# Column sums of z and of its squares: two TensorE matmuls for each two chunks instead of VectorE's additions

## The reference, cut to what matters

```python
messages = jnp.concatenate([node_rep[src], edge_rep[dst]], axis=-1)
messages = _bn_relu(messages @ W1, g1, b1)        # z = messages @ W1, 50000 x 256
# _bn_relu: mu = mean(z, axis=0), var = var(z, axis=0), relu((z - mu) * rsqrt(var + 1e-5) * gamma + beta)
edge_new = segment_sum(messages, dst)
```

## Time and profile before

| | us |
|---|---|
| median of three executions | 3559.73 |
| the profiled execution, own time | 3567.03 |
| its span, first to last instruction | 3565.2 |
| PE matmuls busy in it | 2424.9 (68%) |
| DVE busy | 2395.4 (67%) |
| POOL busy | 1734.6 (49%) |
| ACT busy | 1352.5 (38%) |

### The profile page before, as it was taken

One profiled execution on the slowest core, in us unless ns is written; L12 is line 12 of the kernel. 1 busy time (PEld: TensorE's weight loads), 2 busy tenths in 40 slices (PEclk: granted clock), 3 DMA queues, 4 the chain that ended last, 5 costly groups with the idle time before them and its releaser, 6 DMA issues. The chain is left out here.

```text
span 3565.2 us, 41686 instructions
## 1 busy us (share of the span) xinstructions
PE 2424.9 (68%) x12339; PEld 1976.6 (55%) x12339; DVE 2395.4 (67%) x4693; ACT 1352.5 (38%) x2800; POOL 1734.6 (49%) x1269
## 2 busy tenths in 40 slices
PE   4668733454555543666621999879999999925998
PEld 3522213454444443444421897469888988923788
DVE  5979945777777778877886544344565566615788
ACT  2268833444444441000000435424434434423776
POOL 0257887776667667888888777730000000042000
PEclk9779865555555555888855999889999999966999
DMA  9993224665555656555533774146545645340355
GB/s 373 351 355 34 22 26 130 174 171 164 165 165 166 172 170 137 133 142 134 143 40 39 202 177 89 1 103 185 175 126 172 185 130 173 118 103 8 109 173 176
DMA packets 338453, 517.84 MB, mean 145 GB/s; under 512 B 145379, under 2 KB 227100, under 8 KB 331580
## 3 DMA queue, kind: packets, MB, share of 16 engines
q1 hardware_dynamic: 190254, 436.41, 38.2%
q0 software_dynamic: 134768, 58.41, 14.2%
q10 hardware_dynamic: 13214, 20.35, 1.7%
HBM read 369.65 MB, written 145.38 MB: 144 GB/s over the span
## 5 line engine op out<-in xcount | busy, mean ns | idle before, releaser
L1133 PE MATMUL banks<-rows_r,lhs_r 128*128 128x448 f32 x3500 | 899.1, 372 | 84.0 <-issue 41.6
L728 POOL DMA_INDIRECT counts<-wts x391 | 637.4, 1630 | 307.9 <-DMA counts<-ring 141.0
L1133 PEld LDWEIGHTS banks<-rows_r,lhs_r 128*128 128x128 f32 x3500 | 667.8, 191 | 152.9 <-issue 74.8
L741 POOL DMA_INDIRECT weights<-wts x391 | 620.9, 1588 | 161.8 <-issue 159.1
L1133 PE MATMUL banks<-ring_r,lhs_r 128*128 128x448 f32 x1750 | 525.8, 370 | 0.0
L749 POOL DMA_INDIRECT reg<-tab_p,w x416 | 406.9, 978 | 217.9 <-issue 122.8
L548 DVE SCALAR_TENSOR_TENSOR ring_r<-ring,dinv,rows_r 128x896 fp32r<-128x896 f32 (+1 forms) x300 | 303.7, 1033 | 309.5 <-ACT rows_r L535 309.3
L1221 PE MATMUL banks<-lhs_r,oT 128*128 x416 | 203.3, 489 | 429.8 <-issue 346.6
L535 ACT ACTIVATE rows_r<-ring,dinv 128x896 fp32r<-128x896 f32 (+1 forms) x300 | 285.0, 951 | 399.3 <-PE banks L1133 342.0
L799 POOL DMA_INDIRECT el<-tab_l,base_i x25 | 24.0, 958 | 796.8 <-DMA tab_l<-reg 789.5
L1221 PEld LDWEIGHTS banks<-lhs_r,oT 128*128 128x128 f32 x416 | 131.9, 317 | 447.3 <-issue 447.0
(11 more groups left out here) (269 smaller groups left out, 4104.6 us busy)
## 6 DMA issues: line engine op xcount, KB each, us to landing
ring<-weights SPq DMA_DIRECT2D x225, 448.0 KB
ring<-counts SPq DMA_DIRECT2D x150, 448.0 KB
zbuf<-reg SPq DMA_DIRECT2D x208, 256.0 KB
reg<-zbuf SPq DMA_DIRECT2D x52, 1024.0 KB
counts<-ring SPq DMA_DIRECT2D x25, 1568.0 KB, 16.4
weights<-ring SPq DMA_DIRECT2D x25, 1568.0 KB
ring<-weights SPq DMA_DIRECT2D x75, 224.0 KB
dr<-low_rows_d SPq DMA_DIRECT2D x52, 256.0 KB
```

Of the source, the lines that this page charges most:

```text
L728: pool.indirect_dma_start(counts, bass.IndirectOffsetOnAxis(ap=ix_c[:, k:k + 1], axis=0), vals_c[:, k:k + 1], None, compute_op=ALU.add).th ...
L741: pool.indirect_dma_start(weights, bass.IndirectOffsetOnAxis(ap=ix_w[:, k:k + 1], axis=0), vals_w[:, k:k + 1], None, compute_op=ALU.add).t ...
L1133: m = pe.matmul(bank[:, 0:BLK], lhs[part], rows[:, c:c + BLK], start=first, stop=last)
```

## The change

TensorE takes the sums over as it goes. For each unit, two units behind, `sum_z` on PE multiplies `ones` (128 x 128, f32) with the 128 x 512 f32 tile of z into bank 6 and with that of the squares into bank 7; both banks accumulate over all 208 units. The calls stand behind the matmuls of `add_q(q)` and ahead of `degrees`. DVE's `sum_z`, the copy L1630 and the eight matmuls L1248 with their semaphores are gone; two waits are new, ACT's before it overwrites a tile of squares and DVE's before it overwrites a tile of z, both on `z_summed`. Since a bank holds two chunks side by side, DVE adds the two halves in four instructions where it had two. SyncE's wait for `stat_done` before the third load of the message stage is gone.

```diff
@@ scalar, z stage
                     act.wait_ge(z_ready, q + 1)
+                    wait(act, z_summed, q - SQ + 1)
                     act.activation(zsq[q % SQ], zz[q % ZS], ACT.Square).then_inc(sq_ready, 1)
@@ tensor
+            def sum_z(q):
+
+                pe.wait_ge(sq_ready, q + 1)
+                for bank, z in ((ps[6], zz[q % ZS]), (ps[7], zsq[q % SQ])):
+                    m = pe.matmul(bank[:, :], ones[:, :], z, start=(q == 0), stop=(q == KQ - 1), skip_group_check=True)
+                m.then_inc(z_summed, 1)
+
             def add_q(q):
...
                 m.then_inc(zq_done, 1)
+                if q >= 2:
+                    sum_z(q - 2)
...
-            pe.wait_ge(z_acc, KQ + 1)
-            for part in range(2):
-                for k in range(2):
-                    o = (2 * part + k) * H
-                    m = pe.matmul(stat_bank[:, part * H:(part + 1) * H], ones[:, :], zsum[:, o:o + H], start=(k == 0), stop=(k == 1))
-            m.then_inc(stat_done, 1)
+            sum_z(KQ - 2)
+            sum_z(KQ - 1)
@@ vector, z stage
                 v.wait_ge(zq_done, q + 1)
+                wait(v, z_summed, q - ZS + 1)
                 wait(v, z_stored[q // 2 % (ZS // 2)], 32 * (q // ZS))
...
-            def sum_z(q):
-
-                v.wait_ge(sq_ready, q + 1)
-                if q == 0:
-                    v.tensor_copy(zacc2, z_both(0)).then_inc(z_acc, 1)
-                    return
-                v.wait_ge(z_acc, q)
-                v.tensor_tensor(zacc2, zacc2, z_both(q), ALU.add).then_inc(z_acc, 1)
...
-                    if q >= 2:
-                        sum_z(q - 2)
...
-            v.tensor_copy(zsum, zacc).then_inc(z_acc, 1)
...
-            v.wait_ge(stat_done, 1)
-            do(v.tensor_scalar(mean_t, stat_bank[:, 0:H], 1.0 / E, None, ALU.mult))
+            v.wait_ge(z_summed, KQ)
+            do(v.tensor_scalar(mean_t, ps[6][:, 0:H], 1.0 / E, None, ALU.mult))
+            do(v.scalar_tensor_tensor(mean_t, ps[6][:, H:2 * H], 1.0 / E, mean_t, ALU.mult, ALU.add))
+            do(v.tensor_scalar(sq_t, ps[7][:, 0:H], 1.0 / E, None, ALU.mult))
+            do(v.scalar_tensor_tensor(sq_t, ps[7][:, H:2 * H], 1.0 / E, sq_t, ALU.mult, ALU.add))
             do(v.tensor_tensor(var_t, mean_t, mean_t, ALU.mult))
-            do(v.scalar_tensor_tensor(var_t, stat_bank[:, H:2 * H], 1.0 / E, var_t, ALU.mult, ALU.subtract))
+            do(v.tensor_tensor(var_t, sq_t, var_t, ALU.subtract))
```

More of the change, by code:

```diff
@@ L297, in gnn_kernel @@
         assert (ZS + SQ) * 2 * H <= 24 * H
-        def z_both(q):
-            return view(Z_AT + q % ZS * 2 * H, 2, (ZS + q % SQ - q % ZS) * 2 * H)[:, :, 0:2 * H]
-        zsum = view(F0, 4 * H)
         dr = [typed(f"dr{k}", reg_at + 4 * (F0 + 32 * H) + 2 * k * 8 * P, 8 * P, BF16) for k in range(2)]
@@ L311, in gnn_kernel @@
         hot_d = [view(F0 + k * 8 * P, 8, P) for k in range(2)]
-        var_t, mean_t = view(F0, H), view(F0 + H, H)
+        var_t, mean_t, sq_t = view(F0, H), view(F0 + H, H), view(F0 + 2 * H, H)
         uT, h2T, h3T = view(RD, JH, NP), view(RE, 2 * JH, NP), view(RD, JH, NP)
@@ L401, in gnn_kernel @@
         pair_bank_w = (ps[1], ps[6])
-        deg_bank, tot_bank, stat_bank, sort_bank = ps[0], ps[1], ps[4], (ps[4], ps[5])
+        deg_bank, tot_bank, sort_bank = ps[0], ps[1], (ps[4], ps[5])
         mask, cols_ps = banks[:, 2 * 512:2 * 512 + NG * P], banks[:, 2 * 512 + NG * P:4 * 512]
-        nb_ps, zacc = ps[2][:, 0:H], banks[:, 6 * 512:8 * 512]
+        nb_ps = ps[2][:, 0:H]
         assert NG * P + P == 2 * 512
@@ L432, in gnn_kernel @@
         dr_loaded = [sem(f"dr_loaded{k}") for k in range(2)]
-        oT_ready, zq_done, z_ready, sq_ready, z_acc = names("oT_ready", "zq_done", "z_ready", "sq_ready", "z_acc")
+        oT_ready, zq_done, z_ready, sq_ready, z_summed = names("oT_ready", "zq_done", "z_ready", "sq_ready", "z_summed")
         z_stored = [sem(f"z_stored{k}") for k in range(ZS // 2)]
-        stat_done, bn_var, bn_std, edge_bn, deg_var, deg_std, abs_a, a_cols, gT_scaled = names(
-            "stat_done", "bn_var", "bn_std", "edge_bn", "deg_var", "deg_std", "abs_a", "a_cols", "gT_scaled")
+        bn_var, bn_std, edge_bn, deg_var, deg_std, abs_a, a_cols, gT_scaled = names(
+            "bn_var", "bn_std", "edge_bn", "deg_var", "deg_std", "abs_a", "a_cols", "gT_scaled")
         z_loaded = [sem(f"z_loaded{k}") for k in range(3)]
@@ L621, in _ @@
                 sp.wait_ge(z_stored[s], 32 * len(range(s, KQ // 2, ZS // 2)))
-            sp.wait_ge(z_acc, KQ)
+            sp.wait_ge(z_summed, KQ)
             def load_pair(i):
@@ L633, in _ @@
             for i in range(NPASS):
-                if i == 2:
-                    sp.wait_ge(stat_done, 1)
                 if i >= 3:
@@ L1600, in add_z @@
                                 gp[:, k:k + 2, :].rearrange("p a c -> p (a c)"), ALU.add).then_inc(z_ready, 1)
-            zacc2 = zacc.rearrange("p (a b) -> p a b", a=2)
-            def sum_z(q):
-                v.wait_ge(sq_ready, q + 1)
-                if q == 0:
-                    v.tensor_copy(zacc2, z_both(0)).then_inc(z_acc, 1)
-                    return
-                v.wait_ge(z_acc, q)
-                v.tensor_tensor(zacc2, zacc2, z_both(q), ALU.add).then_inc(z_acc, 1)
             destination_T(0)
@@ L1626, in _ @@
                         equal_cells(SORT_G + n // NG, n % NG)
-            sum_z(KQ - 2)
-            sum_z(KQ - 1)
-            v.wait_ge(z_acc, KQ)
-            v.tensor_copy(zsum, zacc).then_inc(z_acc, 1)
             v.memset(en, 0.0)
```

## The result

The changed kernel took 3762.43 us, median of four executions (3761.05 to 3769.64); the kernel before, beside it, 3558.68 us. The ratio is 1.0587, 95% interval 1.0558 to 1.0616. The forecast was 3750 us. The profiled execution of the changed kernel took 3761.05 us, 194 us more than that of the kernel before (3567.03 us); the prediction's sum said +190.

What follows compares the result with a forecast made beforehand. POOL's list was taken to bound the kernel until 2354 us. 48 passes * (20.0 - 15.95) = +194, less 4, gave 3567.0 + 190 = 3757 us profiled; the median, 7.3 lower, 3750 us, range 3600 to 3940.

Steps and rivals of the forecast that it cites:

- the prediction's sum: Whole kernel: 48 passes growing from 15.95 to 20.0 us give +194, less 4 at the end: +190 us.
- POOL's list sets the end: Up to 2354 us POOL's instruction list sets the end; each microsecond POOL loses in the z stage moves it by one.
- The ring: Z stage, 48 passes: square, sum, degree matmul, ACT's steps, next square form a closed round, 3.83 us high clock, 5.8 low.
- The hand-over from ACT to PE: From the square's end to the next sum's start on PE: 0.25 us taken, between 0.06 and 0.56.
- The register reads: Once a pass PE's eight reads wait for the pending sum's release; the stretch takes 6.6 us.
- The clock: PE's granted clock in the z stage would be 0.83, a third of the time low, making a round 4.33 us.
- the clock stays low all through: Rival, chance 0.12: PE's clock stays low in the z stage, a pass takes 24.0 to 24.4 us, +392, 3950 us.
- A pass and the sum: Z stage: three rounds, one stretch with reads and 0.4 us for total matmuls make 20.0 us a pass; over 48 passes, +194.
- The reads are hidden: Rival, chance 0.12: PE's reads run under the wait, a pass takes 15.7 us, 3548 us; up to 17.3, +61, partly low.
- Faster: Rival, chance 0.07: DVE's additions delayed L1599, so a pass falls to POOL's 14.0 us, 97 us less, 3462.
- The bound of 97 us: Most that relief of the z stage could bring: 1.95 us a pass over 50 passes.
- PE's wait for the square: Sign expected in the new trace: PE's new line waits for ACT's square about 1 us a unit.

Runs made afterwards that it cites:

- e1: The changed kernel with PE's sum of unit q-2 put behind the degree matmuls instead of ahead, chip 10: 3562.65 us, 1.0316 of the kernel before.
- e9: The changed kernel with PE's sums three units behind instead of two, at the same place, chip 8: 3610.33 us, 1.0165 of the kernel before.
- e7: The changed kernel with sums over 256 columns of each tile only, except first and last unit, chip 10: 3606.82 us, 1.0448 of the kernel before.
- e2: The changed kernel with two register reads in each unit instead of eight per pass, chip 10: 3521.52 us, 1.0193 of the kernel before.
- e5: The kernel before, unchanged, run again on chip 10 for its trace: 3455.41 us, ratio 0.9999.
- e8: The kernel before with DVE's z additions narrowed to columns 0 to 63, chip 10: 3457.14 us, 1.0006 of the kernel before.
- e10: The changed kernel with sums three units behind and two register reads in each unit, chip 8: 3562.77 us, 1.0016 of the kernel before.
- e11: The kernel before, unchanged, a third time, on chip 8, one execution: 3546.14 us.
- e3: The changed kernel with sums behind the degree matmuls and two register reads in each unit, chip 10: 3457.94 us, 1.0007 of the kernel before.
- e4: The kernel before with two register reads in each unit instead of eight per pass, DVE's additions kept, chip 10: 3454.19 us, ratio 1.0000.

## Why the prediction was right, point by point

**POOL's list sets the end: right.** +203 us at the last gather (1367.7 us before, 1570.2 after), +198 at `dense(1)`, +194 at the end.

**The ring: right.** The links were predicted at 1.72 + 0.4 + 1.46 + 0.25 = 3.83 us and measured 1.82 + 0.42 + 1.46 + 0.05 = 3.75. At the low level 5.8 was predicted, 5.5 measured. Opened in two ways (e1, e9) it vanished, and halving its first link (e7) shortened it by 0.85 us, nearly half of the link. The hand-over from ACT to PE lies at the lower bound: 0.25 should have been near the 0.06 of the row that is itself a hand-over the earlier trace rows.

**The register reads: right, and a little short.** They start at 905.4, when the sum that had waited is released (905.23), and the stretch takes 7.4 us where 6.6 was taken. Their other condition, DVE's addition of unit 4i-2, had been met 1.1 to 6.3 us before their start in the passes behind the first four, so it is not what held them. In nine of 48 passes, those with the small total matmuls ahead of the reads, they start 2.59 us behind the sum's start and not 0.13; over all passes that is 0.5 us, and 0.4 was added for it. By the rule of the Trainium skill that was weighed against this (Perfetto Trace Analysis, section "Tensor Engine Instruction (MATMUL, LD_WEIGHTS)"), the sequencer decodes on under a pending matmul, and a pass would have been about 15.7 us; here it is 20.4, and the reads did not pass the pending wait. Where they differ the measurement decides. Spreading the reads gave back 228 us (e2).

**The clock: right in size.** The stage's windows, 560 to 1580 us, show 0.85 where 0.83 was taken:

```profile
560.00:1580.00 1020.00, 722.96 (x3367) 441.39 (x3368) 394.85 (x1100) 340.36 (x980) 569.05 (x511) 0.85 0.47 133
```

One round of a pass is slow, the one behind the pause; without the pause all are fast (e2, 0.99). The Trainium skill describes this (TensorE: Matmul & The Clock Gate, section "HAM oscillation"): a burst after a pause starts cold. The trace agrees for the first sum, 3.62 us against 1.98. The rival that the prediction put beside it, by which the clock stays low all through, did not come about.

**A pass and the sum.** 20.4 us measured in 600 to 1290 us, 20.0 predicted. The three rounds are as forecast (5.5 + 3.75 + 3.75 = 13.0, and 3 * 4.33 = 13.0); the stretch with the reads makes the difference, 7.4 against 6.6 + 0.4. Over the whole stage the gathers take 1025.9 us (544.3 to 1570.2) against 822.8 before: +203, with passes a little shorter at the end than in that window, where the sum had +190. From there on the difference shrinks, to +200 at POOL's last addition into `weights`, +198 at `dense(1)` and +194 at the end. What gives these 9 us back no run shows; executions of the changed kernel lie as far apart (3761 to 3770 us). It is not DVE's relief at the end of the stage: DVE starts its first clearing 13.0 us behind the last gather (1583.15) where it was 19.9, but POOL waits for none of that, and the prediction was right to put it at nothing. The mechanism and its size were forecast well; that 190 came within 4 us of 194 is luck: the sum was 13 us short for the stage, and 9 us came back behind it.

**The rivals.** "The reads are hidden" is close to e2, where the long pause is gone: had they been hidden, the time would be near e2's. "Faster" rested on 1.9 us a pass in which POOL waits for L1599, and on DVE's additions as the possible reason. The row was read rightly; the reason is, as far as the runs go, PE's slow spells: where they are missing the wait is 0.3 us a pass (e5), and DVE's relief changes nothing there (e8). On chip 8 e10 has neither DVE's additions nor the long pause, and its pass is still 15.9 us, so the additions were hardly the reason there either; e8 itself was not run on it. The bound of 97 us holds only where a pass takes 15.95: on chip 10 next to nothing was to be had.

**In the list of signs** one was off: PE's wait for the square was to be about 1 us a unit; PE's row of waits gives 56.6 / 136 = 0.4 (up to 0.85 in a fast round), since a slow round leaves PE hardly any idle time.

**Open.** What the slow spells are, and why the kernel before and e10 have them on chip 8, e9 few there in the z stage, and the changed kernel none in the first comparison. The traces show an engine that issues slowly or whose results come late, and no cause. Of the 91 us between e11 and e5 (spans 3544.3 and 3453.7 us) 80 have arisen by the last gather (1355.9 and 1275.8), the rest behind the stage. No version tried beats the kernel before; e3 and e4 are within 0.2% of it. With a pass at 14.1 us on chip 10, against POOL's own 14.00, what is left to gain in this stage is POOL's list itself; that was not tried.

## What to carry to other kernels

Before moving work onto an engine that has room, write down the order in which it stands there and what each neighbour waits for. An instruction that waits for a late product, put ahead of one for which that product's maker waits, closes a ring, and then its full length counts in every round (here 1.82 of 3.75 us a unit) however idle both engines look. Let it ask for something one unit older, or put it behind, and look at what the engine's sequencer does between (register reads) as a second, separate cost; either fault alone is enough to lose the time.

## What the runs showed of the hardware

- A pending wait of a matmul held up the eight register reads behind it; they began 0.2 us after its release and took 6.2 us up to the following matmul's start (905.4 to 911.60).
- The same kernel with the same work took 3455 us on one chip and 3558 on another, with an equal duration of the single gather (973 and 976 ns) and the same clock in the z stage (0.50). On the slower one PE had short spells in which it started an instruction only every 0.7 or 1.4 us, or in which its results came 1.5 to 7.2 us behind the recorded end of the matmul.
- At the low clock level (0.50 in 912.70 to 916.00 us) the sum of four 512-column matmul instructions took 3.62 us, at the high (1.00 in 918.20 to 927.00 us) 1.98; the granted clock was 0.50 in the z stage of the kernel before, with a pause of 5 to 7 us in each pass, and 0.99 in e2's, without the long pause.
